# Later sends in the plan, and a third place for activations, in a two-layer attention and mixture-of-experts kernel

## The chip, the cores and the metric

One core of a Trainium2 chip runs the whole program in one launch. The metric is the device time of that core in microseconds (us); lower is better. The engines are TensorE (PE), VectorE (DVE), ScalarE (ACT), GpSimd (POOL) and SyncE (SP), which issues most of the transfers. Each takes its instructions from a queue of its own in a fixed order.

## The reference

The input x has 8 sequences of 512 rows with 128 columns. Two layers follow. In each, attention with 16 heads is added to x and then a mixture of experts. All is float32.

```python
x = x + attn_a(layernorm(x))     # 16 heads, 8 + 32 query and key columns, softmax
x = x + ffn(layernorm(x))
x = x + attn_b(layernorm(x))     # rotary q and k, softmax(q1 k1) - lam * softmax(q2 k2)
x = x + ffn(layernorm(x))

def ffn(x):                      # 8 experts, 512 hidden, the best expert of each row alone
    score = softmax(x @ Wg + bg); e = argmax(score)
    h = silu(x @ W1[e] + b1[e])
    return (h @ W2[e] + b2[e]) * score[e]
```

## The kernel before, in words

**Batches and groups.** A batch b is one sequence in one layer: 16 of them, 0 to 7 for the first attention and 8 to 15 for the second. A batch of the first has 4 groups g and one of the second 8, 96 groups in all. For a group, smax (L1238) computes scores, rowmax on DVE (L1587) their maxima, score (L1259) computes them again transposed, expo on ACT (L1461) exponentiates, pv (L1271) multiplies with the values. The stack stage (SP, L1050) loads a group's q and k from DRAM, the mput stage its maxima. After a batch come normal, join (POOL, L1852), oproj, a second layer norm (ln_stats on DVE, ln_rstd L1810 and ln_apply L1530 mostly on POOL), gating, and scatter (POOL, L1861), which sends rows by indirect transfer to their expert's region in DRAM (`xs`). In the second layer POOL also does the rotary products (turned, L1833 to L1839) and splits into halves (b_lo, L1845).

**Expert blocks.** The 16 batches form four segments (3, 5, 6 and 2 batches). When a segment's batches are scattered, its rows are worked off in blocks m of 128 rows: 19, 27, 31 and 15 blocks, 92 in all (77 before the tail). A block's stages are:

- weights (SP, L1068 and L1063): 576 KB of one expert, into one of seven places WE
- rows (SP, L1105; its waits are at L1104): 128 rows into X, six places. It waits until the send of block m - 6 has landed.
- xturn (PE, L1344), xcopy (ACT, L1491), up (PE, L1352)
- silu_t (ACT, L1500): tanh of up's result into TH; it waits for the down of block m - 2, as Z and TH have two places each
- either on POOL, for the 46 blocks for which `on_pool` holds (segment 1, and segment 2 without its last twelve, the late blocks): silu_z (ACT, L1509) copies up's result into Z, silu_p (POOL, L1868 and L1870) makes two passes over 128x512, down (PE, L1367), weigh (ACT, L1506), plus_p (POOL, L1876)
- or, for the other blocks: silu_b (DVE, L1753), down, combine (DVE, L1760)
- plus_b2 (DVE, L1747), and send (POOL, L1883): an indirect transfer of the 128 finished rows to DRAM (`x2` after layer one, `out` after layer two). It waits for plus_p or combine.

The tail (15 blocks) has six places of Z and TH, in other memory. `mixed` uses the first two places of TH early on, to prepare the experts' weights.

**The order of the work.** It isn't written by hand. `schedule()` is a planner: coroutines (jobs) ask for stages, each with a rank, and the planner places them one at a time. `STAGES` (L193 to L210) holds each stage's engine and planned duration in us, `HOP` what passes until another engine sees the result, `LANDS` how long a transfer takes to land after its issue. For each engine it takes the stage that can start first, with the lower rank on a tie (PE alone weighs rank in, by 0.08 us each), and then the earliest over all engines. Every placement moves the engine's clock, and so what is placed next. Out of it come the orders of the five queues and the PSUM banks, which are then emitted as code; on the chip the engines wait by semaphore and keep these orders, whatever the durations really are. Waits that the plan makes among stages are `after(...)`. In `expert(m)` up is asked for after the down of block m - `back_z`, which is 2 before the tail and 6 in it. Five jobs (lanes) work off the blocks before the tail, block m + 5 after block m's send has been placed. In `step` a stage that follows another of its job on the same engine is ready when that engine is free (`free`), on another engine when the result is seen (`ready`).

Of the kernel before, what the change touches and what calls it, by code (L numbers as in the profile page):

```python
# [7 lines left out]
F32 = mybir.dt.float32  # L8
# [37 lines left out]
M0 = TAIL[0]  # L46
# [101 lines left out]
def weight_slot(m):  # L148

    if m < M0:  # L150
        return m % 7
    return f"t{m - M0}" if m < M0 + 5 else (m - 5) % 7
# [16 lines left out]
def late(m):  # L169

    return M0 - 12 <= m < M0


def on_pool(m):

    return 0 < BLOCKS[m][0] < NS - 1 and not late(m)
# [10 lines left out]
def ends_of_segment(k):  # L187
# [16 lines left out]
    "expo": ("scalar", 0.49), "mcopy": ("scalar", 0.18), "ocopy": ("scalar", 0.49), "hcopy": ("scalar", 0.49), "raw": ("scalar", 0.5), "fhi": ("scalar", 0.585),  # L204
    "vcopy": ("scalar", 0.58), "b_hi": ("scalar", 1.05), "acopy": ("scalar", 0.49), "gcopy": ("scalar", 0.49),
    "gate_exp": ("scalar", 0.25), "silu_z": ("scalar", 0.48), "weigh": ("scalar", 0.265), "plus_p": ("gpsimd", 0.46), "mix": ("vector", 1.4), "wsum": ("tensor", 0.86), "silu_t": ("scalar", 0.49), "lambda_exp": ("scalar", 0.25),
    "index": ("gpsimd", 0.2), "ln_rstd": ("gpsimd", 1.36), "turned": ("gpsimd", 7.4), "silu_p": ("gpsimd", 2.64), "b_lo": ("gpsimd", 2.27), "scatter": ("gpsimd", 4.9), "send": ("gpsimd", 1.0),
    "xload": ("sync", 0.6), "setup": ("sync", 0.6), "put": ("sync", 1.8), "direct": ("sync", 3.6), "stack": ("sync", 1.2), "mput": ("sync", 0.6), "weights": ("sync", 1.1),
    "rows": ("sync", 1.1), "blank": ("sync", 0.6), "fill": ("sync", 9.0), "weights_b": ("sync", 0.6), "weights_p": ("sync", 0.6),
    "wload": ("sync", 1.0), "wstore": ("sync", 0.6),  # L210
# [23 lines left out]
def schedule(ticks=False):  # L234
# [12 lines left out]
    def after(*events):  # L247
        yield ("after", events)

    def do(rank, stage, *index, us=None, engine=None):  # L250
        yield from behind(stage, index)
        yield ("do", rank, stage, index, 0, us, engine)

    def fill_bank(rank, stage, *index, us=None):
        yield from behind(stage, index)
        yield ("do", rank, stage, index, 1, us, None)
# [16 lines left out]
    def find_banks(n, t, stage):  # L273

        kind = stage if stage in MOST else "other"
        held = sum(1 for bank in RB if bank not in idle and (holder[bank][0] if holder[bank][0] in MOST else "other") == kind)
        most = len(RB) if ("scored", (NG - 1,)) in ended else MOST[kind]
        if held >= most:
            return None
        pair, single = free_banks(2) if n == 2 and held + 2 <= most else None, free_banks(1)  # L280
        if single is None:
            return None
        if n == 2 and held > 1 and kind == "smax":
            return pair
        return pair if pair and pair[0] <= max(t, single[0]) else single
# [24 lines left out]
    def give(stage, *index):  # L310
        for bank, _ in ring[stage, index]:
            idle[bank] = ended[LAST[0]]
# [308 lines left out]
    def rank_of(m):  # L621
        k, i = BLOCKS[m]
        return FROM[k][0] + FROM[k][1] * i
# [40 lines left out]
    def lane(ms):  # L664
        for m in ms:
            yield from expert(m)

    def expert(m):
        rank, tail = rank_of(m), BLOCKS[m][0] == NS - 1
        first, back_z = (M0, 6) if tail else (0, 2)  # L670
        if late(m):
            rank = 95.9 + 0.1 * (m - M0 + 12)
            yield from after()
        yield from after(("rows", (m,)), ("weights", (m,)))
        yield from fill_bank(rank, "xturn", m)
        if m >= 4:
            yield from after(("up", (m - 4,)))
        yield from do(rank, "xcopy", m)
        give("xturn", m)
        spawn(plus(m, rank))  # L680
        if m - back_z >= first:
            yield from after(("down", (m - back_z,)))
        yield from fill_bank(rank, "up", m)
        if m == M0:
            yield from after(("pv", (NG - 1, 3)))
        yield from do(rank, "silu_t", m)
        if on_pool(m):
            yield from do(rank, "silu_z", m)
            give("up", m)
            yield from do(rank, "silu_p", m)  # L690
        else:
            yield from do(rank, "silu_b", m)
            give("up", m)
        yield from fill_bank(rank, "down", m)
        yield from after(("plus_b2", (m,)))
        if on_pool(m):
            yield from do(rank, "weigh", m)
            give("down", m)
            yield from do(rank, "plus_p", m)
        else:  # L700
            yield from do(rank, "combine", m)
            give("down", m)
        yield from do(rank, "send", m)

    def plus(m, rank):
        yield from do(rank, "plus_b2", m)
# [6 lines left out]
    def step(job, t):  # L713

        while True:
            ask = next(job, None)
            if ask is None:
                return
            if ask[0] == "do":
                _, rank, stage, index, bank, us, engine = ask  # L720
                engine = engine or STAGES[stage][0]
                before, ready, free = last_of.get(job, (None, 0.0, 0.0))
                t = max(t, free if before == engine else ready)
                asked[engine].append((rank, t, job, stage, index, bank, STAGES[stage][1] if us is None else us))
                return
            events = ask[1] if ask[0] == "after" else (ask[1],)
            missing = [e for e in events if e not in ended]
            if missing:
                blocked.setdefault(missing[0], []).append((job, t, ask))
                return  # L730
            if ask[0] == "after":
                t = max([t] + [ended[e] for e in events])

    def spawn(job):
        step(job, now[0])
# [21 lines left out]
    while any(asked.values()):  # L757
        best = None
        for e in ENGINES:
            mine = None  # L760
            for k, (rank, t, job, stage, index, bank, us) in enumerate(asked[e]):
                if bank:
# [3 lines left out]
                    t = max(t, found[0])  # L766
# [14 lines left out]
        rank, t, job, stage, index, bank, us = asked[e].pop(k)  # L781
        if bank:
            _, first, n = find_banks(bank, max(t, clock[e]), stage)
# [35 lines left out]
def build(nc, a):  # L819
    with ExitStack() as ctx:  # L820
        def sb(name, shape, dt):
            return ctx.enter_context(nc.sbuf_tensor(name, shape, dt))
# [52 lines left out]
        X = sb("X", [128, 6, ROWW], F32)  # L875
        XT = sb("XT", [128, 4, 128], F32)
        WE = sb("WE", [128, 7, WEW], F32)
        Z = sb("Z", [128, 2, 512], F32)
        mean = sb("mean", [128, 128], F32)
        TH = sb("TH", [128, 2, 512], F32)  # L880

        xs = [nc.dram_tensor(f"xs{i}", [NE * REG + 128, ROWW], F32, kind="Internal").ap() for i in range(NS)]
        x2 = nc.dram_tensor("x2", [T, D], F32, kind="Internal").ap()
# [9 lines left out]
        def sem(name):  # L893
            if name not in sems:
                sems[name] = ctx.enter_context(nc.semaphore(name))
            return sems[name]
# [30 lines left out]
        def block_place(m):  # L927

            sk, t, xt_ = STK[:, :].bitcast(F32), m - M0, XT[:, m % 4, :]
            if t < 0:  # L930
                return WE[:, m % 7, :], X[:, m % 6, :], xt_, Z[:, m % 2, :], TH[:, m % 2, :]
            zt = P[:, :, :, :].rearrange("p z j n -> p (z j n)")
            w_ = sk[:, 2412 + WEW * t:2412 + WEW * (t + 1)] if t < 5 else WE[:, weight_slot(m), :]
            return (w_, sk[:, ROWW * (t % NE):ROWW * (t % NE + 1)], xt_, zt[:, 512 * (t % 6):512 * (t % 6) + 512],
                    zt[:, 3072 + 512 * (t % 6):3584 + 512 * (t % 6)])

        def z_before(m):

            return m - 2 if m < M0 else m - 6 if m - 6 >= M0 else None

        def xt_before(m):
            return m - 4
# [33 lines left out]
        def bank_of(stage, *index):  # L976

            return ring[stage, index][0][0], [freed(before[0], *before[1]) for _, before in ring[stage, index] if before]
# [4 lines left out]
        def _(eng):  # L983
# [86 lines left out]
            def wload(e):  # L1070
# [3 lines left out]
                if e >= 7:  # L1074
                    on.wait_ge("wst0", 16)
                eng.dma_start(WE[:, e % 7, :], a["we"][128 * e:128 * e + 128, :]).then_inc(sem(f"wl{e % 2}"), 16)
                eng.dma_start(TH[:, e % 2, :], a["b1"][e].rearrange("(a n) -> a n", a=1).broadcast_to([128, FH])).then_inc(
                    sem(f"wl{e % 2}"), 16)
# [92 lines left out]
        def _(eng):  # L1171
# [169 lines left out]
            def xturn(m):  # L1341
                bank = bank_for("xturn", m)
                on.wait_ge(*x_sem(m))
                eng.transpose(ps[:, bank, 0:128], block_place(m)[1][:, 0:128], idf[:, :]).then_inc(sem("ft"), 1)  # L1344
# [189 lines left out]
        def _(eng):  # L1534
            on = On(eng)

            def mix(e):

                on.wait_ge("ws", e + 1)
                eng.scalar_tensor_tensor(out=TH[:, e % 2, :], in0=TH[:, e % 2, :], scalar=1.0 / 128, in1=ps[:, bank_of("wsum", e)[0], :],  # L1540
                                         op0=ALU.mult, op1=ALU.add).then_inc(sem("mix"), 1)
                on.wait_ge("mix", 2 * e + 1)
                eng.tensor_tensor(WE[:, e % 7, 0:FH], WE[:, e % 7, 0:FH], TH[:, e % 2, :], ALU.add).then_inc(sem("mix"), 1)

# [424 lines left out]
```

## Time and profile before

| | us |
|---|---|
| median of 3 runs | 1557.32 |
| lowest and highest | 1546.62, 1561.79 |
| the profiled execution | 1556.93 |
| its span | 1555.1 |

The span runs from the first to the last instruction of the profiled execution; its mean granted TensorE clock is 0.955 of full speed. Busy time of an engine leaves out what only issues or waits, except that POOL's indirect transfers count. In a row of the timeline the bracket at the end is the idle time of that engine before the instruction, and what ended it.

### The profile page before, as it was taken

The page shows a single profiled execution, that of the slowest core. Times are in us where ns is not written, and L with a number is a line of the kernel's source. Part 1 is how long each engine was busy: PE and PEld are TensorE (multiplying, and loading weights), DVE is VectorE, ACT ScalarE, POOL GpSimd, SP SyncE. Part 2 cuts the span into 40 slices and gives each one's busy share as a digit, 9 for nine tenths or more (in the row PEclk, how much of TensorE's full clock was granted, in tenths as well). Part 3 has the DMA queues.
Part 4 walks back from the last instruction along what each step waited for, and adds up shares of the span by engine and source line. Part 5 has one row for each costly group of instructions (what it writes and reads, how often), then busy time and mean ns, then how long its engine had stood idle before and what let it go on. Part 6 is the DMA issues. An engine that isn't in the chain of part 4 may idle for free.

```text
span 1555.1 us, 26964 instructions
## 1 busy us (share of the span) xinstructions
PE 1404.0 (90%) x9162; PEld 604.7 (39%) x9162; DVE 1186.0 (76%) x2033; ACT 1070.9 (69%) x1960; POOL 677.5 (44%) x744
## 2 busy tenths in 40 slices
PE   7989999999999988889988889889998998889986
PEld 3323334334554322445442323223233323443376
DVE  6757688887778677866669899898988987668563
ACT  3556566676666766778677788787888866767832
POOL 5332344334413861587755543514343123854043
PEclk8999999999999988999899999999999977999998
DMA  2488576865762243545301542211211135533073
GB/s 82 128 263 248 166 226 188 268 189 177 221 189 76 79 145 121 174 143 166 109 28 35 154 140 77 70 34 56 56 42 55 29 100 173 168 120 99 2 252 91
DMA packets 125230, 199.81 MB, mean 128 GB/s; under 512 B 16728, under 2 KB 91186, under 8 KB 125094
## 3 DMA queue, kind: packets, MB, share of 16 engines
q1 hardware_dynamic: 115910, 184.23, 39.8%
q0 software_dynamic: 6016, 12.71, 2.4%
q10 hardware_dynamic: 3168, 1.15, 0.3%
q8 instruction: 74, 1.21, 0.3%
q14 instruction: 62, 0.51, 0.1%
HBM read 123.90 MB, written 72.59 MB: 126 GB/s over the span
## 4 chain that ended last, share of the span: by engine, by line
PE 56%; ACT 11%; POOL 10%; DVE 9%; issue 6%; SPq 3%; DMA 3%; ACTq 1%; another core or an unknown queue 0%; POOLq 0%; DVEq 0%
PE ps L1271 17%; PE ps L1238 10%; PE ps L1259 9%; ACT P L1461 8%; DVE Mb L1587 7%; PE ps L1367 4%; PE ps L1352 3%; PE ps L1204 3%; PE ps L1279 2%; POOL TH L1868 2%; POOL Z L1870 2%; PE ps L1324 1%; POOL x L1883 1%; PE ps L1220 1%; PE ps L1305 1%
## 5 line engine op out<-in xcount | busy, mean ns | idle before, releaser
L1587 DVE TENSOR_REDUCE Mb<-ps 128x2 f32<-128x1024 f32 (+1 forms) x993 | 921.3, 976 | 203.7 <-PE ps L1238 189.7
L1461 ACT ACTIVATE P<-ps 128x512 f32<-128x512 f32 (+1 forms) x1275 | 797.4, 693 | 204.3 <-PE ps L1259 168.0
L1259 PE MATMUL ps<-STK 32*128 32x512 f16 (+1 forms) x1536 | 403.5, 392 | 40.5 <-ACT P L1461 28.0
L1271 PE MATMUL ps<-P,V 128*32 128x512 f32 x3072 | 416.2, 625 | 0.7 <-ACT OR L1468 0.2
L1238 PE MATMUL ps<-STK 32*128 32x512 f16 (+1 forms) x1536 | 371.0, 392 | 35.8 <-ACT P L1461 11.9
L1238 PEld LDWEIGHTS ps<-STK 32*128 32x128 f16 (+1 forms) x1536 | 99.9, 93 | 322.5 <-DVE Mb L1587 104.5
L1259 PEld LDWEIGHTS ps<-STK 32*128 32x128 f16 (+1 forms) x1536 | 108.9, 94 | 225.4 <-ACT P L1461 105.2
L1271 PEld LDWEIGHTS ps<-P,V 128*32 128x32 f32 x3072 | 65.8, 110 | 129.5 <-issue 112.6
L1861 POOL DMA_INDIRECT xs<-ROW,slot x64 | 63.7, 995 | 103.8 <-DVE slot L1678 88.6
L1367 PE MATMUL ps<-WE,Z 128*128 128x128 f32 x616 | 92.5, 297 | 17.7 <-POOL Z L1870 12.8
L1825 POOL CAST HL<-RT 128x512 f16<-128x512 f32 x47 | 28.8, 612 | 171.0 <-ACT RT L1407 150.9
L1367 PEld LDWEIGHTS ps<-WE,Z 128*128 128x128 f32 x616 | 80.7, 204 | 50.2 <-issue 20.9
L1352 PE MATMUL ps<-XT,WE 128*128 128x128 f32 x696 | 97.0, 285 | 3.0 <-ACT XT L1491 1.7
L1352 PEld LDWEIGHTS ps<-XT,WE 128*128 128x128 f32 x696 | 87.5, 197 | 20.6 <-issue 8.2
L1852 POOL TENSOR_TENSOR AT<-AT,OT 128x256 f32<-128x256 f32 x32 | 23.4, 732 | 157.5 <-DVE OT L1610 157.2
L1868 POOL TENSOR_TENSOR TH<-TH,Z 128x512 f32<-128x512 f32 x46 | 58.6, 1274 | 70.9 <-ACT Z L1509 70.1
L1883 POOL DMA_INDIRECT x<-X x46 | 46.3, 1006 | 95.7 <-DVE X L1760 74.3
L1500 ACT ACTIVATE TH<-ps 128x512 f32<-128x512 f32 x77 | 46.2, 601 | 57.1 <-PE ps L1352 50.3
L1204 PE MATMUL ps<-HT,WA 128*128 128x512 f32 x158 | 83.0, 623 | 1.3 <-ACT HT L1390 0.6
L1530 POOL TENSOR_SCALAR ROW<-ROW,mv,rs 128x128 f32<-128x128 f32 x100 | 78.3, 792 | 2.0
L1833 POOL TENSOR_TENSOR RT<-RT,CS 128x512 f32<-128x512 f32 x32 | 40.6, 1276 | 84.2 <-ACT RT L1417 84.0
L1279 PE MATMUL ps<-idf,OR 128*128 128x128 f32 x320 | 53.2, 291 | 9.7 <-ACT P L1461 5.6
(160 smaller groups left out, 1378.8 us busy)
## 6 DMA issues: line engine op xcount, KB each, us to landing
WE<-wx SPq DMA_DIRECT2D x87, 576.0 KB, 4.0
STK<-qka SPq DMA_DIRECT2D x56, 480.0 KB
qka<-HL SPq DMA_DIRECT2D x84, 256.0 KB, 4.8
STK<-qkb SPq DMA_DIRECT2D x64, 256.0 KB
qkb<-HL SPq DMA_DIRECT2D x96, 128.0 KB, 2.7
X<-xs SPq DMA_DIRECT2D x77, 129.5 KB
xs<-pad SPq DMA_DIRECT2D x8, 1036.0 KB
qka<-HL SPq DMA_DIRECT2D x42, 128.0 KB
```

Source lines behind the costliest of these rows:

```text
L1204: eng.matmul(ps[:, bank, :], WA[:, 128 * x:128 * x + 128], HT[:, b % 2, :], start=True, stop=True).then_inc(sem("pr"), 1)
L1238: mm = eng.matmul(ps[:, bank + i, :], l_, r_, start=True, stop=True)
L1259: mm = eng.matmul(ps[:, bank + i, :], l_, r_, start=True, stop=True)
L1271: mm = eng.matmul(ps[32 * j:32 * j + 32, OB, :], V[:, b % 3, kt, at:at + 32], P[:, st % 3, j, :], start=(kt == 0 and (b >= B or hh % 2 == ...
L1279: mm = eng.transpose(ps[:, bank, 128 * i:128 * i + 128], OR[:, 128 * i:128 * i + 128], idf[:, :])
L1352: mm = eng.matmul(ps[:, bank, 128 * c:128 * c + 128], w_[:, 128 * c:128 * c + 128], xt_, start=True, stop=True)
L1367: mm = eng.matmul(ps[:, bank, 0:128], z[:, 128 * c:128 * c + 128], w_[:, FH + D * c:FH + D * c + D], start=(c == 0), stop=(c == 3))
L1461: eng.activation(P[:, st % 3, j:j + n, :], ps[:, bank:bank + n, :], ACT.Exp, scale=SCALE_A if g < 4 * B else SCALE_B).then_inc(sem("exp"), 1)
L1530: eng.tensor_scalar(ROW[:, t0 + i, 0:128], ROW[:, t0 + i, 128:256], mv[:, z, i, 0:1], rs[:, z, i:i + 1], ALU.subtract, ALU.mult).then_inc( ...
L1587: eng.tensor_reduce(Mb[:, g % 2, at:at + 4 * n - 3:4], ps[:, bank:bank + n, :], AX, ALU.max).then_inc(sem("mx"), 1)
L1861: eng.indirect_dma_start(out=xs[k][:, :], out_offset=bass.IndirectOffsetOnAxis(ap=slot[:, t:t + 1], axis=0), in_=ROW[:, t, 0:ROWW], in_off ...
L1868: eng.tensor_tensor(th, th, z, ALU.mult).then_inc(sem("fq"), 1)
```

## The change

Four things change. The planned duration of send goes from 1.0 to 1.2 us. The planner takes a send as ready 0.65 us later than its operand. Z and TH have three places each instead of two for the blocks before the tail (2 KB more for each in every partition). So silu_t waits for the down of block m - 3, and the planner asks for up after that same down. No instruction is added or removed on the chip; the orders of the queues come from a new run of the planner.

```diff
-    ... "send": ("gpsimd", 1.0),
+    ... "send": ("gpsimd", 1.2),
@@ def expert(m)
-        first, back_z = (M0, 6) if tail else (0, 2)
+        first, back_z = (M0, 6) if tail else (0, 3)
@@ def step(job, t)
-                t = max(t, free if before == engine else ready)
+                t = max(t, free if before == engine else ready) + (0.65 if stage == "send" else 0.0)
@@ def build(nc, a)
-        Z = sb("Z", [128, 2, 512], F32)
+        Z = sb("Z", [128, 3, 512], F32)
-        TH = sb("TH", [128, 2, 512], F32)
+        TH = sb("TH", [128, 3, 512], F32)
@@ def block_place(m)
-                return WE[:, m % 7, :], X[:, m % 6, :], xt_, Z[:, m % 2, :], TH[:, m % 2, :]
+                return WE[:, m % 7, :], X[:, m % 6, :], xt_, Z[:, m % 3, :], TH[:, m % 3, :]
@@ def z_before(m)
-            return m - 2 if m < M0 else m - 6 if m - 6 >= M0 else None
+            return m - 3 if m < M0 else m - 6 if m - 6 >= M0 else None
```

## Rows read from the trace of the kernel before

**Rows 1.** The page: busy time of two engines, and POOL's tenths in 40 slices.

```profile
PE 1404.0 (90%) x9162; PEld 604.7 (39%) x9162; DVE 1186.0 (76%) x2033; ACT 1070.9 (69%) x1960; POOL 677.5 (44%) x744
...
POOL 5332344334413861587755543514343123854043
```

**Rows 2.** Busy time by stretch: engines in columns, then PE clock, DMA share, GB/s.

```profile
core 0: us, PE busy (x) PEld busy (x) DVE busy (x) ACT busy (x) POOL busy (x), PEclk, DMA share, GB/s
200.00:350.00 150.00, 147.04 (x845) 57.35 (x847) 125.69 (x239) 102.62 (x165) 55.62 (x66) 1.00 0.72 216
350.00:480.00 130.00, 128.46 (x846) 72.76 (x842) 95.62 (x164) 81.52 (x134) 45.38 (x52) 1.00 0.61 179
636.00:676.00 40.00, 35.35 (x280) 21.03 (x272) 28.38 (x35) 31.85 (x63) 33.12 (x33) 1.00 0.52 159
676.00:706.00 30.00, 25.70 (x178) 13.33 (x178) 19.30 (x26) 21.68 (x40) 25.22 (x25) 0.89 0.43 129
706.00:726.00 20.00, 18.88 (x151) 10.68 (x149) 13.90 (x19) 15.42 (x34) 16.36 (x17) 1.00 0.56 169
...
1302.00:1362.00 60.00, 52.71 (x406) 30.51 (x399) 39.42 (x55) 44.56 (x90) 48.09 (x49) 0.98 0.50 153
```

**Rows 3.** The chain that ended last, by line: 636 to 680, then 1302 to 1362.

```profile
by line: POOL TH L1868 23.2%; POOL Z L1870 23.1%; issue 18.8%; POOL x L1883 16.5%; POOL X L1876 9.1%; PE ps L1352 2.5%; PE ps L1271 2.3%; POOL AT L1852 1.7%; ACT Z L1509 1.3%; ACT TH L1500 1.0%; POOLq L905 0.6%; POOLq L1883 0.6%
...
by line: POOL Z L1870 23.2%; POOL TH L1868 23.1%; issue 17.0%; POOL out L1883 17.0%; POOL X L1876 8.2%; POOL AT L1852 3.7%; PE ps L1271 3.1%; PE ps L1352 2.2%; ACT Z L1509 1.0%; ACT TH L1500 0.7%; PE ps L1344 0.7%; POOLq L905 0.6%; POOLq L1
```

**Rows 4.** Order of time on POOL: start, duration, instruction, idle time before it.

```profile
648.89 1.28 POOL L1868 TENSOR_TENSOR TH<-TH,Z 128x512 f32<-128x512 f32 x1
...
651.48 0.46 POOL L1876 TENSOR_TENSOR X<-X 128x128 f32<-128x128 f32 x1
652.71 1.00 POOL L1883 DMA_INDIRECT x<-X  x1 [0.77 <-POOL X L1876]
653.75 1.28 POOL L1868 TENSOR_TENSOR TH<-TH,Z 128x512 f32<-128x512 f32 x1
```

**Rows 5.** Who waited for whom: us in total, times, longest.

```profile
POOL x L1883 <- POOL X L1876: 18.7, 24, 0.8
...
PE ps L1367 <- POOL Z L1870: 12.8, 16, 2.8
...
POOL out L1883 <- POOL X L1876: 12.8, 16, 0.8
```

**Rows 6.** Order of time on PE, ACT, POOL and SP's queue, 659 to 682.

```profile
659.11 0.27 PE L1344 MATMUL ps<-idf,X 128*128 128x128 f32 x1
...
669.65 0.62 ACT L1509 COPY Z<-ps 128x512 f32<-128x512 f32 x1
...
673.31 1.28 POOL L1868 TENSOR_TENSOR TH<-TH,Z 128x512 f32<-128x512 f32 x1
...
677.12 1.01 POOL L1883 DMA_INDIRECT x<-X  x1 [0.77 <-POOL X L1876]
...
681.51 3.51 SPq L1105 DMA_DIRECT2D X<-xs  x2
```

**Rows 7.** Order of time on POOL: sends that don't follow the stage they wait for.

```profile
407.56 1.11 POOL L1883 DMA_INDIRECT x<-X  x1 [0.18 <-issue]
...
1477.55 0.76 POOL L1852 TENSOR_TENSOR AT<-AT,OT 128x256 f32<-128x256 f32 x1
1478.48 0.99 POOL L1883 DMA_INDIRECT out<-X  x1 [0.17 <-issue]
```

**Rows 8.** What SP's queue waited for at the rows stage.

```profile
SPq L1104 <- DMA x<-X: 47.4, 20, 5.7
SPq L1104 <- DMA out<-X: 31.3, 17, 4.2
```

**Rows 9.** The chain in order of time, late blocks: start, us, what.

```profile
1491.95 3.98 DMA X<-xs
```

**Rows 10.** Groups of instructions by line: xturn on PE.

```profile
L1344 PE MATMUL ps<-idf,X 128*128 128x128 f32 x77 | 21.1, 289 | 1.8 <-DMA X<-xs 1.8
```

More of the change, by code:

```diff
@@ L206 @@
     "gate_exp": ("scalar", 0.25), "silu_z": ("scalar", 0.48), "weigh": ("scalar", 0.265), "plus_p": ("gpsimd", 0.46), "mix": ("vector", 1.4), "wsum": ("tensor", 0.86), "silu_t": ("scalar", 0.49), "lambda_exp": ("scalar", 0.25),
-    "index": ("gpsimd", 0.2), "ln_rstd": ("gpsimd", 1.36), "turned": ("gpsimd", 7.4), "silu_p": ("gpsimd", 2.64), "b_lo": ("gpsimd", 2.27), "scatter": ("gpsimd", 4.9), "send": ("gpsimd", 1.0),
+    "index": ("gpsimd", 0.2), "ln_rstd": ("gpsimd", 1.36), "turned": ("gpsimd", 7.4), "silu_p": ("gpsimd", 2.64), "b_lo": ("gpsimd", 2.27), "scatter": ("gpsimd", 4.9), "send": ("gpsimd", 1.2),
     "xload": ("sync", 0.6), "setup": ("sync", 0.6), "put": ("sync", 1.8), "direct": ("sync", 3.6), "stack": ("sync", 1.2), "mput": ("sync", 0.6), "weights": ("sync", 1.1),
```

## The prediction

> **What bounds the kernel now.** I read the page first. PE is busy for 90% of the span and POOL for 44% [rows 1]. So TensorE looks like the bound and GpSimd like an engine with room. But the digits of the 40 slices show that POOL's share is uneven: it is 8, 7, 7 tenths in the slices from about 660 to 780 us and 8 again around 1320 to 1360, which are the stages in which the expert blocks of segments 1 and 2 run beside attention. Those are the blocks that the change touches, so the second view is busy time by stretch [rows 2]. In the two stretches before the third stage, 200 to 350 us and 350 to 480 us (there segment 0 runs its blocks on VectorE), PE is busy for 98.0% and 98.8%: nothing is to be had. In 636 to 676 us PE falls to 35.35 of 40 us (88%), in 676 to 706 to 25.70 of 30 (86%), in 706 to 726 to 18.88 of 20 (94.4%), in 1302 to 1362 to 52.71 of 60 (88%). POOL is busy for 33.12 of 40 and 48.09 of 60 there.
>
> The third view is the chain that ended last, cut to these stretches [rows 3]: from 636 to 680 us POOL's own lines and "issue" make up over 90% of it, and the same from 1302 to 1362. The fourth is POOL's order of time [rows 4]. One turn is silu_p (L1868, L1870), plus_p (L1876), send (L1883), from the silu_p at 648.89 to the next at 653.75: 4.86 us. In it POOL stands still for 0.77 us between plus_p, which writes the rows, and the send that waits for them. The whole list of waits has 24 + 16 = 40 such gaps, 18.7 + 12.8 = 31.5 us, and PE waits at down (L1367) for POOL's Z 16 times, 12.8 us [rows 5]. So in these stretches the bound is a saturated POOL, in front of a PE with some 12% to spare.
>
> **The change, part by part.** Two edits are to the planner. A send is planned at 1.2 us instead of 1.0, and as ready 0.65 us after its operand. The old plan has a send begin at once behind its plus_p, at 2.64 + 0.46 + 1.0 = 4.10 us for a block; the chip takes 4.86. The new plan sees, at the end of plus_p, a send that is ready only 0.65 us later; any other POOL stage that is ready before that is placed first. What is that? In the trace the next block's silu_p: its Z was copied at 669.65 to about 670.27, two turns ahead of need by the order, and POOL comes to it at 673.31, behind a send (1.00 us and its gap of 0.77) [rows 6]. Without that send POOL would come at 671.5, so Z is ready in time with two places already, by about 1 us, and with three places easily, as its up no longer waits for the down just made. I expect the order silu_p, send of the block before, plus_p.
>
> What is the gap then? The trace has sends whose operand was long there and that follow some other instruction; two of them show 0.18 and 0.17 us idle [rows 7]. The two ends for the gap in the new place are thus 0.17 (a saving of 0.60) and 0.77 (no saving, if the lead belongs to the send itself); I take 0.20, by these rows, the nearest in kind: a saving of 0.57 us for each.
>
> A rule speaks against this. The Trainium skill, "Perfetto Trace Analysis", section "DMA Instruction — SWDGE (GPSIMD)", says that such an instruction has no start marker, only an end, when the last DSP has made its descriptors. By that the 0.77 us could be part of the send's own work and would move with it: no saving, 1557. What the trace shows goes against it: from the end of plus_p at about 651.94 to the next silu_p at 653.75 are 1.81 us, while the send at 1478.48 ends 1.16 us after the join before it ended [rows 4, 7].
>
> How many gaps count? In 636 to 676 there are 7, in 676 to 706 4, in 706 to 726 4, in 1302 to 1362 11: 26 of the 40. The other 14 lie where POOL waits for ACT or stands beside a PE that is already full, and I cost them at nothing; PE's work hides them. For the 26, POOL gives 4.0, 2.3, 2.3 and 6.3 us. What is late next is PE: at the 98% of [rows 2] its 35.35 us need 36.1, so at most 3.9 us go; in 706 to 726 at most 0.7; in 1302 to 1362 52.71 need 53.8, at most 6.2. In 676 to 706 the long rotary stages stand on POOL's chain and half of 2.3, 1.1, is what I count. Sum 11.9 us. If PE gets only to the 94.4% that it had in 706 to 726, the terms are 2.6, 1.1, 0 and 4.2: 7.9 us. I take the middle, 9.9.
>
> The third place of Z and TH. On the blocks on POOL it is what lets up and tanh run a block ahead; priced above. On the 19 blocks of segment 0 it is worth nothing, since PE is full there (98.8%). On the twelve late blocks the chain shows a row load of 3.98 us at 1491.95 [rows 9], which a place of Z doesn't shorten: between 0 and 4 us (if an earlier up hid it all), taken as 0, since the row names the load. The tail already has six places.
>
> The later send. It frees X's slot (six of them) for the rows of six blocks on, and SP stands for it in its one queue: 20 + 17 waits, 47.4 + 31.3 us [rows 8]. One block followed through: xturn at 659.11, its send at 677.12, and the rows that take its slot are issued from 681.51, 4.4 us after the send; add 4 us to land [rows 9]: 685.5, a life of 26.4 us [rows 6]. Six turns of 4.86 are 29.2. The new order adds a silu_p, 2.6 us, and the six turns shrink by 6 x 0.57 = 3.4; that asks for 6.0 where 2.8 is free behind the rows. The rest has to come out of the waits inside the life (Z stands 3.0 us before silu_p takes it, 670.27 to 673.31, and part of the time between xturn and up is a wait too). They hold about the 3.2 us that are missing, hence a cost of 0; the other end is the whole gain lost.
>
> All other order is planned anew too, as each placement moves those behind it. No row prices that; the three times of before span 1546.6 to 1561.8, so a plan that is a little better or worse somewhere is hard to tell from a run. I leave it at 0 with 8 us to either side.
>
> **Sum.** The profiled execution took 1556.93 us (span 1555.1), the median of the runs shown is 1557.32, so both stand for the same. 1556.9 - 9.9 = 1547.0 us.
>
> **The rivals.**
> (a) No gain, by X's ring or PE. If the waits inside a block's life don't shrink, the turn is (26.4 + 2.6) / 6 = 4.83 us, what it is now. The same comes out if the send stays behind its plus_p, or if the lead is the send's own and moves with it (the Trainium skill's missing start marker, above); that alone I hold for 0.05 of the 0.22. For it: SP's 37 waits for a send. Against it: PE waited at xturn (L1344) for X's rows for 1.8 us in the whole trace [rows 10]. Time 1556.
> (b) The plan fits, and all 40 gaps count: 40 x 0.57 = 22.8 us, with PE's 16 waits for Z inside that. For it: the old plan was 0.76 us a block too fast, so everything that it put behind was late too. Against it: the PE limit above. Time 1534.
> (c) Slower: SP's queue. Each rows stage waits until its send has landed, some 2 us later than now, and behind it on SP stand the stack (the q and k of a later group, L1050) and the weights (L1068). It decides when the stack's slack is used up: in the two stages, 320 us together, some 23 groups start (the second layer's 64 take about 870 us, 13.6 each); if for each smax is 2 us late and none of POOL's gain is left, that is 46 us, if for half, 23. Against it: the planner places the stack 3.4 groups ahead of its use, some 40 us at the pace of the second layer, and 2 us of that matter little. Time 1556.9 + 23 = 1580.
>
> **How the numbers follow.** Forecast 0.53, (a) 0.22, (b) 0.13, (c) 0.12. The forecast's own range is 1539 to 1555 with the replanning. Leaving out the outer half of (c) and a little of (b), the range is 1532 to 1566. One per cent, 15.6 us, is about what a measurement of this kernel tells from no change, given its spread: faster means under 1541.7. To that go (b) and about two fifths of the forecast, 0.34. Slower, over 1572.9, is most of (c): 0.10. The rest is 0.56.
>
> **What would show it.** Right: POOL's order of time around 640 to 680 us has send behind silu_p with 0.2 us idle before it; the waits of L1883 for POOL's X fall from 40 to a few; a turn takes 4.3 to 4.5 us; PE is busy for 94 to 98% from 636 to 676 and from 1302 to 1362; the last send to x2 comes earlier. Wrong: a gap of 0.7 us before a send that follows silu_p (the lead is the send's own); turns of 4.8 us with xturn waiting for rows (a); SP's waits at L1104 well over 80 us and DVE or PE waiting for a stack (c); or turns as forecast and the time unchanged, with PE's idle time moved to 750 to 850 or to the end.

## The result, and the profile after

The changed kernel takes 1515.31 us in the median of 4 runs (1514.28 to 1524.05). The kernel before, run beside it, has a median of 1553.37 (4 runs). The ratio is 0.9759, 95% interval 0.9719 to 0.9800: faster by 2.4%. The forecast was 1547.0 us (0.994), with a range from 1532 to 1566, so the time lies outside the range, on the faster side. The profiled execution took 1515.25 us; its span is 1513.4, 41.7 us less than that of before.

The page of the changed kernel, busy time by engine and POOL's tenths in 40 slices:

```profile
PE 1382.8 (91%) x9162; PEld 594.7 (39%) x9162; DVE 1188.0 (78%) x2046; ACT 1070.1 (71%) x1958; POOL 678.6 (45%) x744
...
POOL 5332334424422764387865643414433133964143
```

Beside [rows 1], POOL's, DVE's and ACT's busy times are the same to within 2 us. PE's is 21.2 us shorter with the same 9162 matmuls. PE's idle time went from 1555.1 - 1404.0 = 151.1 to 1513.4 - 1382.8 = 130.6 us, 20.5 us less. So the gain has two halves, and my working has terms only for the second. Part of the first half belongs to the two executions and not to the kernels: the profiled one of before had a mean granted clock of 0.955, that of the changed kernel 0.970, and the last section shows what such a difference goes with in one kernel.

The step of the forecast that was about POOL came out as written. Order of time on POOL, changed kernel (start, duration, instruction, idle time before it), which answers to [rows 4]:

```profile
637.99 1.27 POOL L1868 TENSOR_TENSOR TH<-TH,Z 128x512 f32<-128x512 f32 x1
639.34 1.27 POOL L1870 TENSOR_TENSOR Z<-Z,TH 128x512 f32<-128x512 f32 x1
640.76 1.01 POOL L1883 DMA_INDIRECT x<-X  x1
641.79 0.47 POOL L1876 TENSOR_TENSOR X<-X 128x128 f32<-128x128 f32 x1
642.20 1.28 POOL L1868 TENSOR_TENSOR TH<-TH,Z 128x512 f32<-128x512 f32 x1
```

The send stands behind the next block's silu_p, 0.15 us after it, and a turn takes 4.21 us where it took 4.86. The waits of the changed kernel (us, times, longest), which answer to [rows 5] and [rows 8], and the group of xturn, to [rows 10]:

```profile
POOL x L1883 <- POOL X L1876: 3.9, 5, 0.8
...
POOL out L1883 <- POOL X L1876: 0.8, 1, 0.8
```

```profile
SPq L1104 <- DMA x<-X: 46.0, 17, 8.2
SPq L1104 <- DMA out<-X: 37.1, 15, 4.8
```

```profile
L1344 PE MATMUL ps<-idf,X 128*128 128x128 f32 x77 | 21.8, 293 | 0.6 <-DMA X<-xs 0.3 <-ACT Z L1509 0.2
```

Six gaps are left of 40. The wait of down for POOL's Z, 12.8 us before, is not in the list any more. SP stands 83.1 us for sends instead of 78.7, and PE waits for X's rows for 0.3 us: X's ring held.

The chain that ended last, changed kernel, from 628 to 672 us, then from 1274 to 1340 ([rows 3] before), and busy time in two stretches at the head of the two stages ([rows 2]):

```profile
by line: PE ps L1352 20.8%; PE ps L1367 17.1%; PE ps L1271 14.5%; DVE Mb L1587 13.5%; PE ps L1238 7.0%; DVE X L1747 6.4%; issue 5.8%; PE ps L1259 5.6%; PE ps L1344 2.1%; PE ps L1279 2.0%; PE ps L1204 2.0%; ACT P L1461 1.4%; PE ps L1244 1.1%
...
by line: PE ps L1367 23.3%; PE ps L1352 20.2%; PE ps L1271 19.4%; PE ps L1238 11.0%; PE ps L1259 7.4%; ACT P L1461 4.8%; DVE Mb L1587 2.9%; ACT TH L1500 2.2%; PE ps L1344 2.2%; PE ps L1279 2.2%; ACT Z L1509 1.6%; issue 1.2%; PE ps L1244 0.9
```

```profile
628.00:668.00 40.00, 38.41 (x299) 21.31 (x295) 32.23 (x45) 34.07 (x69) 37.05 (x36) 1.00 0.50 151
1284.00:1344.00 60.00, 57.44 (x453) 31.28 (x451) 46.03 (x64) 49.26 (x100) 50.90 (x54) 1.00 0.57 171
```

POOL is gone from the chain and PE has taken its place, busy for 96.0% and 95.7% where it was at 88%; I had written 94 to 98%.

**Where the other half lies.** To compare the same work in two traces I cut them at the ACT copies L1468, which end the groups. There is one for every group of the second layer and one for every two of the first, so number 15 (of 80, counted from 0) is the last of layer one. The copies with the numbers 15, 31, 63, 71 and 79 bound four stretches. Three of them in the kernel before (segment 1's stage, the middle, the first part of segment 2's stage), then in the changed kernel:

```profile
core 0: us, PE busy (x) PEld busy (x) DVE busy (x) ACT busy (x) POOL busy (x), PEclk, DMA share, GB/s
568.77:847.69 278.92, 245.19 (x1700) 113.74 (x1696) 202.03 (x327) 200.10 (x387) 166.75 (x174) 0.90 0.38 120
847.69:1227.91 380.22, 342.86 (x2466) 112.68 (x2465) 341.65 (x543) 312.16 (x583) 146.98 (x151) 1.00 0.25 72
1227.91:1373.66 145.75, 128.24 (x850) 57.52 (x847) 105.47 (x176) 99.53 (x196) 68.98 (x71) 0.87 0.42 130
```

```profile
565.35:820.40 255.05, 230.37 (x1683) 107.85 (x1679) 201.35 (x340) 197.24 (x387) 162.13 (x168) 0.95 0.43 131
820.40:1204.28 383.88, 350.35 (x2485) 113.04 (x2483) 345.35 (x551) 315.73 (x596) 151.71 (x157) 0.99 0.25 71
1204.28:1329.84 125.56, 116.12 (x828) 53.07 (x825) 101.95 (x166) 95.91 (x196) 67.34 (x68) 0.93 0.47 144
```

Segment 1's stage is 23.9 us shorter: PE idles 9.1 us less and is busy 14.8 us less. Segment 2's is 20.2 us shorter: 8.1 us of idle time and 12.1 of busy time. The middle gives 3.7 us back: PE is busy there for 7.5 us more, with 19 more matmuls, so a part of the shorter busy time is work that has moved to another stretch. In both stages the granted clock is higher, 0.90 to 0.95 and 0.87 to 0.93. The clock doesn't sag evenly: it drops to half speed (1.2 GHz) for some microseconds. One such drop in the kernel before, 4 us a line:

```profile
752.00:756.00 4.00, 2.81 (x18) 0.64 (x18) 2.44 (x4) 3.26 (x7) 4.00 (x5) 0.89 0.18 45
756.00:760.00 4.00, 3.90 (x20) 1.25 (x19) 2.28 (x3) 1.69 (x5) 3.92 (x6) 0.50 0.55 156
760.00:764.00 4.00, 4.00 (x21) 3.16 (x21) 2.25 (x7) 2.46 (x5) 2.06 (x2) 0.50 0.01 1
764.00:768.00 4.00, 4.00 (x28) 1.21 (x27) 1.72 (x5) 2.86 (x5) 1.56 (x2) 0.50 0.35 94
768.00:772.00 4.00, 4.00 (x37) 3.47 (x38) 1.23 (x9) 1.98 (x5) 1.27 (x2) 0.90 0.56 172
```

Before it PE was busy for only 2.81 of 4 us, while POOL was busy for 4.00 of 4; afterwards PE is full and slow for some 12 us. What PE waited for just before the drop, and what ACT had waited for:

```profile
752.35 0.38 PE L1259 MATMUL ps<-STK 32*128 32x512 f16 x1 [0.92 <-ACT Z L1509]
753.72 0.39 PE L1238 MATMUL ps<-STK 32*128 32x512 f16 x1 [0.84 <-ACT P L1461]
...
750.18 1.14 ACT L1424 CAST HL<-RT 128x512 f16<-128x512 f32 x2 [1.06 <-POOL RT L1839]
```

So PE waited for ACT here, and ACT a little earlier for POOL's rotary products, not for a block's silu_p or send. The changed kernel has two such drops after 620 us in segment 1's stage where the kernel before has four. Before all four PE waited for ACT, and in two of them (688 and 752 us) ACT had waited for POOL's rotary products.

### The profile page after: what moved, and what is told of

Its sections match the earlier page's. It is cut to its first block, busy times and chain, and to the rows that moved or that the text cites. A ratio compares the mean times of both kernels' runs of the same rounds, so it can differ in the third digit from the quotient of the medians.

```text
span 1513.4 us, 26975 instructions
## 1 busy us (share of the span) xinstructions
PE 1382.8 (91%) x9162; PEld 594.7 (39%) x9162; DVE 1188.0 (78%) x2046; ACT 1070.1 (71%) x1958; POOL 678.6 (45%) x744
## 4 chain that ended last, share of the span: by engine, by line
PE 66%; DVE 11%; ACT 11%; issue 5%; SPq 2%; POOL 2%; DMA 2%; ACTq 1%; another core or an unknown queue 0%; POOLq 0%; DVEq 0%
PE ps L1271 19%; PE ps L1259 11%; PE ps L1238 11%; DVE Mb L1587 9%; ACT P L1461 7%; PE ps L1367 6%; PE ps L1352 6%; PE ps L1204 3%; PE ps L1279 2%; PE ps L1220 1%; PE ps L1324 1%; PE ps L1305 1%; ACT OR L1468 1%; PE ps L1244 1%; PE ps L1344 1%
## 5 line engine op out<-in xcount | busy, mean ns | idle before, releaser
L1587 DVE TENSOR_REDUCE Mb<-ps 128x1 f32<-128x512 f32 (+1 forms) x1006 | 922.9, 966 | 167.4 <-PE ps L1238 159.6
L1259 PE MATMUL ps<-STK 32*128 32x512 f16 (+1 forms) x1536 | 395.3, 388 | 34.6 <-ACT P L1461 20.2
L1271 PE MATMUL ps<-P,V 128*32 128x512 f32 x3072 | 409.4, 615 | 1.0 <-ACT OR L1468 0.2
L1367 PE MATMUL ps<-WE,Z 128*128 128x128 f32 x616 | 89.4, 290 | 6.9 <-issue 3.0
L1367 PEld LDWEIGHTS ps<-WE,Z 128*128 128x128 f32 x616 | 77.4, 197 | 36.2 <-issue 15.9
```

Source lines behind the costliest of these rows:

```text
L1259: mm = eng.matmul(ps[:, bank + i, :], l_, r_, start=True, stop=True)
L1271: mm = eng.matmul(ps[32 * j:32 * j + 32, OB, :], V[:, b % 3, kt, at:at + 32], P[:, st % 3, j, :], start=(kt == 0 and (b >= B or hh % 2 == ...
L1367: mm = eng.matmul(ps[:, bank, 0:128], z[:, 128 * c:128 * c + 128], w_[:, FH + D * c:FH + D * c + D], start=(c == 0), stop=(c == 3))
L1587: eng.tensor_reduce(Mb[:, g % 2, at:at + 4 * n - 3:4], ps[:, bank:bank + n, :], AX, ALU.max).then_inc(sem("mx"), 1)
```

## The experiments

Each ran in 4 to 10 executions beside the kernel before on the same chip; the ratios are to that. Their intervals reach 0.003 to 0.008 to either side. Theory A is that POOL's gap was on the path and its going is the gain, B that the new plan of all queues gains, C that the third place does.

**The sends alone, in both directions.** `swap` keeps all orders of the kernel before and, after planning, moves on POOL each send that stands right behind its plus_p one stage back:

```diff
         order, ring = schedule()
+        late_sends, i = order["gpsimd"], 1
+        while i < len(late_sends) - 1:
+            (s0, x0), (s1, x1), (s2, x2_) = late_sends[i - 1:i + 2]
+            if s0 == "plus_p" and s1 == "send" and x0 == x1 and s2 in ("silu_p", "join", "turned"):
+                late_sends[i], late_sends[i + 1] = late_sends[i + 1], late_sends[i]
+                i += 1
+            i += 1
```

> The kernel before with all its orders kept, except that on POOL each send that stood right behind its own plus_p changes places with the stage behind it (silu_p, join or turned). Theory A (the idle 0.77 us between plus_p and send lay on the path): turns of about 4.2 us instead of 4.86 and most of the gain, a ratio of 0.976 to 0.985. Theory B (the new plan of all five queues is what gains, by its order on PE): at most a third of the gain, 0.992 to 1.000. Theory C (the third place gains): 0.997 to 1.003.

`unswap` is the inverse, on the changed kernel:

```diff
         order, ring = schedule()
+        sends = [x for x in order["gpsimd"] if x[0] == "send" and on_pool(x[1][0])]
+        rest = [x for x in order["gpsimd"] if x not in sends]
+        order["gpsimd"] = [y for x in rest for y in ([x, ("send", x[1])] if x[0] == "plus_p" else [x])]
```

> The changed kernel with all its orders and three places kept, except that on POOL each send of a block on POOL is put back right behind its plus_p. Theory A: the gap of 0.77 us and turns of 4.86 us are back and most of the gain is gone, a ratio of 0.990 to 1.000 to the kernel before. Theory B: 0.976 to 0.983, as the changed kernel. Theory C: the same, 0.976 to 0.983.

Measured: swap 0.9880 (0.9799 to 0.9960), 1534.46 us. unswap 0.9919 (0.9880 to 0.9959), 1538.87 us. For unswap theory A's range held and those of B and C didn't; swap fell between the ranges of A and B. Neither theory had it whole. POOL's order in swap, then in unswap (the lines of the file are a few higher):

```profile
642.72 1.27 POOL L1877 TENSOR_TENSOR Z<-Z,TH 128x512 f32<-128x512 f32 x1
644.14 1.01 POOL L1890 DMA_INDIRECT x<-X  x1 [0.15 <-issue]
645.18 0.47 POOL L1883 TENSOR_TENSOR X<-X 128x128 f32<-128x128 f32 x1
645.60 1.27 POOL L1875 TENSOR_TENSOR TH<-TH,Z 128x512 f32<-128x512 f32 x1
```

```profile
655.38 1.27 POOL L1873 TENSOR_TENSOR Z<-Z,TH 128x512 f32<-128x512 f32 x1
656.62 0.45 POOL L1879 TENSOR_TENSOR X<-X 128x128 f32<-128x128 f32 x1
657.85 1.01 POOL L1886 DMA_INDIRECT x<-X  x1 [0.77 <-POOL X L1879]
658.89 1.29 POOL L1871 TENSOR_TENSOR TH<-TH,Z 128x512 f32<-128x512 f32 x1
```

The gap of 0.77 us is tied to the place behind plus_p, under either plan. What down on PE waited for POOL's Z (us, times, longest), swap, then unswap, 12.8 us before:

```profile
PE ps L1374 <- POOL Z L1877: 1.3, 2, 1.1
...
PE ps L1370 <- POOL Z L1873: 12.2, 13, 3.3
```

So with two places too Z comes in time once the sends are moved. And the same stretch between copies 15 and 31, swap, then unswap:

```profile
567.84:827.17 259.33, 232.02 (x1700) 109.56 (x1696) 206.30 (x327) 198.78 (x387) 166.64 (x174) 0.96 0.42 129
```

```profile
569.34:845.74 276.40, 243.06 (x1683) 110.94 (x1679) 203.72 (x340) 197.90 (x387) 162.35 (x168) 0.90 0.40 121
```

Moving the sends alone takes 19.6 us out of this stage under the old plan; putting them back adds 21.4 us under the new. In both PE's busy time goes with them (245.2 to 232.0, and 230.4 to 243.1), and so does the clock, 0.90 without the move and 0.95 or 0.96 with it. These are the two pairs in which the stage moves most; the seven pairs below, and this line of the same stage in replan_b3, a new plan of the kernel before with 38 of the 40 gaps still in it, show that the clock isn't tied to the gaps alone:

```profile
568.02:820.14 252.12, 223.38 (x1678) 105.65 (x1674) 203.52 (x340) 194.95 (x381) 164.90 (x169) 0.99 0.43 132
```

Over the whole kernel the move is worth 0.012 in one plan and 0.016 in the other. The rest of the change, at either place of the sends, is worth 0.008 to 0.012.

**The edits apart.** `plan` has the two planner edits and two places; `places` the three places with the old planner (its weights stage also waits for plus_b2 of the block that held the place of WE).

```diff
 plan:    the 1.2 and the + (0.65 if stage == "send" else 0.0) of the change, nothing else
 places:  back_z, Z, TH, block_place and z_before of the change, and in weights(m)
+                    on.wait_ge("fbp" if on_pool(weight_before(m)) else "fb", nth(weight_before(m)))
```

> The two edits of the planner alone (send ready 0.65 us later and planned at 1.2 us), Z and TH with two places. Theory A: Z was ready about 1 us ahead of POOL with two places, so the new order holds and nearly all of the gain comes, 0.976 to 0.985. Theory C (the third place is needed to let up run ahead): less than half of it, 0.988 to 1.000. Theory B doesn't say: another plan, another time.

> The third place of Z and TH alone (with it the weights stage also waits for plus_b2 of the block that held its place, which this order needs), the planner's send as before. Theory A: POOL's turn stays 4.86 us with its gap of 0.77 us, so 0.995 to 1.003. Theory C: most of the gain, 0.976 to 0.985.

Measured: plan 0.9875 (0.9811 to 0.9940), between the ranges of A and C, and places 1.0073 (1.0034 to 1.0113). With two places the planner's edits leave 13 of the 40 gaps. The third place alone makes the kernel slower, a result outside both expectations; beside plan it seems worth 0.012. It wasn't quite alone: at helper line L905 SP stands in places for plus_b2, 27.4 us in three waits, 26.5 of them between 1400 and 1460 us, a wait that the kernel before doesn't have. What that costs isn't separated. A part worth +0.007 alone and -0.012 in company raised the question what any new plan does to the time.

**New plans that cheapen nothing.** Each is one small number in the table of planned durations; on the chip no instruction is added, removed or changed.

```diff
 replan_b1 (before), replan_a1 (change):  "index": ("gpsimd", 0.2)  -> 0.25
 replan_b2 (before), replan_a2 (change):  "join": ("gpsimd", 0.73)  -> 0.70
```

> The kernel before, planned anew with another duration for one small stage of POOL (index at 0.25 us instead of 0.2), which makes nothing on the chip cheaper. It measures what a new plan alone is worth. Theory A (the gap on POOL and what follows from it) expects 0.995 to 1.005. Theory B (a new plan of all queues can gain a per cent by luck) expects replanned kernels to scatter by 0.01 or more to either side.

> The kernel before, planned anew with join at 0.70 us instead of 0.73. Theory A: 0.995 to 1.005. Theory B: another draw of the same scatter, 0.01 or more from 1 in one of the two.

> The changed kernel, planned anew with index at 0.25 us instead of 0.2. Theory A: the gain stays, 0.972 to 0.980 to the kernel before. Theory B: part of the gain was the luck of one plan, and it falls to 0.983 to 0.990 here or in the other one.

> The changed kernel, planned anew with join at 0.70 us instead of 0.73. Theory A: 0.972 to 0.980. Theory B: 0.983 to 0.990 here or in the other one.

| | ratio | interval |
|---|---|---|
| replan_b1 | 0.9953 | 0.9918 to 0.9987 |
| replan_b2 | 1.0046 | 1.0000 to 1.0092 |
| replan_a1 | 0.9969 | 0.9931 to 1.0008 |
| replan_a2 | 1.0076 | 1.0040 to 1.0111 |

The two replans of before stay inside theory A's range (0.995 to 1.005). The two of the change lie outside both theories' ranges (0.972 to 0.980, and 0.983 to 0.990), on the slow side. The change, planned anew with 0.05 us more for a stage that runs 16 times, loses nearly all of its gain; with join at 0.70 it ends slower than the kernel before. In both, POOL's sends are still moved (9 and 12 of 40 gaps are left). Where does replan_a2 lose it? Its segment 1 stage is nearly as short as the change's (the first line), but the stretch between copies 71 and 79, at the end of segment 2's blocks, takes 119.79 us (the second):

```profile
570.05:829.95 259.90, 234.58 (x1698) 109.67 (x1694) 205.39 (x346) 197.65 (x383) 166.01 (x172) 0.96 0.43 129
1349.46:1469.25 119.79, 105.86 (x732) 46.06 (x729) 75.78 (x124) 84.28 (x165) 41.87 (x46) 0.90 0.25 74
```

The changed kernel needs 101.01 us for it:

```profile
1329.84:1430.85 101.01, 93.04 (x686) 38.24 (x686) 73.00 (x115) 81.16 (x153) 38.28 (x43) 0.97 0.29 87
```

There PE idles 13.9 us instead of 8.0, and runs at 0.90 of its clock instead of 0.97. A further 12.1 us go in the stretch before it, copies 63 to 71: 137.68 us, where the changed kernel takes 125.56. In the places kernel the stretch between copies 71 and 79 is as long, 118.15 us. From copy 79 to the end all kernels take 81 to 86 us, whatever went before.

**The same move under four more plans.** swap_b1 and swap_b2 are replan_b1 and replan_b2 with the edit of swap; unswap_a1 and unswap_a2 are replan_a1 and replan_a2 with the edit of unswap; unswap_plan is plan with it.

> replan_b1 with only POOL's sends moved behind the stage after their plus_p, as in swap. Theory A' (moving the sends gains the same under any plan, about 0.012 to 0.016 of the time, and the rest of the change's gain is the draw of the plan): 0.9953 - 0.014, so 0.978 to 0.985. Theory B (everything is the draw; the move and its gain in swap were an accident of that plan): 0.992 to 1.000.

> replan_b2 with only POOL's sends moved in the same way. Theory A': 1.0046 - 0.014, so 0.987 to 0.994. Theory B: 1.000 to 1.010.

> replan_a1 with only POOL's sends put back right behind their plus_p. Theory A': 0.9969 + 0.014, so 1.007 to 1.014. Theory B: 0.992 to 1.002.

> replan_a2 with only POOL's sends put back right behind their plus_p. Theory A': 1.0076 + 0.014, so 1.018 to 1.025. Theory B: 1.003 to 1.012.

> plan (the planner's edits, two places) with only POOL's sends put back right behind their plus_p. Theory A' (the move gains in any plan where POOL is on the path; mean of the five pairs so far 0.009): 0.9875 + 0.005 to 0.016, so 0.992 to 1.004. Theory B (only the draw): 0.984 to 0.991.

The last two columns are from the profiled execution of each: how much less PE idles, and how much less it is busy, with the sends moved, in the stretches between copies 15 and 31 and between copies 63 and 71 together.

| plan | sends behind plus_p | sends moved | the move gains | PE idle less, us | PE busy less, us |
|---|---|---|---|---|---|
| before / swap | 1.0000 | 0.9880 | 0.0120 | 13.9 | 14.8 |
| replan_b1 / swap_b1 | 0.9953 | 0.9865 | 0.0088 | 2.3 | -1.5 |
| replan_b2 / swap_b2 | 1.0046 | 0.9992 | 0.0054 | 4.4 | 3.5 |
| unswap / the change | 0.9919 | 0.9759 | 0.0160 | 12.8 | 11.8 |
| unswap_a1 / replan_a1 | 1.0074 | 0.9969 | 0.0105 | 10.0 | -7.4 |
| unswap_a2 / replan_a2 | 1.0080 | 1.0076 | 0.0004 | 13.8 | 8.0 |
| unswap_plan / plan | 0.9940 | 0.9875 | 0.0065 | 9.2 | 6.2 |

No pair goes the other way. The mean is 0.0085, and the seven scatter by 0.005 around it, so 0.004 to 0.013 with 95%: 13 us. Theory A' was right in sign and too high in size: its range held for unswap_a1 and unswap_plan and was missed on the low side by the other three, of which unswap_a2 lies in theory B's range. Theory B doesn't hold for the mean of the seven, but in one plan of seven the move is worth nothing that can be seen.

PE's idle time in the two stages falls in all seven, by 9.5 us in the mean (5.2 to 13.7 with 95%). Its busy time falls by 5.1 us in the mean, with an interval from -2.0 to 12.2: over plans, no busy time is shown to go with the sends.

**More draws.** plan_b1 and plan_b2 are plan with index at 0.25 and join at 0.70; replan_a3 and replan_a4 are the change with index at 0.15 and join at 0.76; replan_b3 is the kernel before with index at 0.15.

> The planner's edits with two places, planned anew with index at 0.25 us. Theory P (the third place is worth nothing; plans with two and three places are draws of the same spread): the mean of plan, plan_b1 and plan_b2 lies within 0.007 of 0.9935, the mean of the change and its two replans. Theory C (the third place gains): their mean lies above 1.000.

> The planner's edits with two places, planned anew with join at 0.70 us. Theories P and C as for plan_b1; by P a single value may lie anywhere from 0.976 to 1.008.

> The change, planned anew with index at 0.15 us. Theory L (the change's own plan is a lucky draw, by about 0.015): 0.985 to 1.008. Theory S (the edits themselves gain 0.02 or more, and replan_a1 and replan_a2 were the unlucky ones): 0.972 to 0.982.

> The change, planned anew with join at 0.76 us. Theory L (lucky draw): 0.985 to 1.008. Theory S (the edits themselves gain 0.02 or more): 0.972 to 0.982.

> The kernel before, planned anew with index at 0.15 us. Theory L: a draw around 1.000, 0.990 to 1.010. If it lies at 0.985 or below, draws as good as the change's are had without its edits, and nothing of the gain beyond the moved sends can be given to them.

| planner's send, places | ratios | mean |
|---|---|---|
| as before, two | 1.0000, 0.9953, 1.0046, 0.9882 | 0.9970 |
| as changed, two | 0.9875, 0.9849, 0.9854 | 0.9859 |
| as changed, three | 0.9759, 0.9969, 1.0076, 0.9843, 0.9850 | 0.9899 |

replan_a3 and replan_a4 fall on the edge of theory L's range (0.9843 and 0.9850, where it begins at 0.985) and outside theory S's. replan_b3, 0.9882 (0.9812 to 0.9951), is a better draw than the range expected of it (0.990 to 1.010). The mean of plan, plan_b1 and plan_b2 is 0.9859, just under theory P's range (0.9865 to 1.0005) and far from theory C's (above 1.000). The five plans of the change have a standard deviation of 0.012; its own is the best of them, 0.014 below their mean. All eight plans with the changed send average 0.9884, 0.0086 below the four without. With this scatter that difference alone has an interval from -0.003 to 0.020; it agrees with the pairs, which show it far better. The third place doesn't show: with it 0.9899, without it 0.9859, and that difference is within the scatter. By ratio no other kernel of the study beat the change.

## Why the prediction was wrong

**Right.** POOL's gap and its price: 0.77 us behind plus_p, 0.15 behind silu_p (I took 0.20), 40 gaps reduced to 6. Z ready in time with two places: swap shows it, where PE's wait for POOL's Z falls to 1.3 us. PE as what is late next, at 96%, and a turn a little shorter than I wrote (4.21 us; I had 4.3 to 4.5). X's ring and SP's queue as covers that hold, so rivals (a) and (c) fell. The rule of the Trainium skill that I weighed against the change ("Perfetto Trace Analysis", section "DMA Instruction — SWDGE (GPSIMD)", no start marker) decided nothing: the trace and the pairs show that the idle time depends on what stands ahead of the send. The size too, taken over plans: 9.9 us forecast, 13 us measured for the move (0.0085, 0.004 to 0.013), and 9.5 us for the idle time of PE in the two stages, the only part that the sum counts.

**The step that failed** is "All other order is planned anew too ... I leave it at 0 with 8 us to either side". That term was mis-sized. Replans that change nothing else run from 0.984 to 1.008, and the plans scatter with a standard deviation of 0.007 for the kernel before and 0.012 for the change, 11 and 19 us, where I had 8 at most. In the change's own plan it came out as 0.008 (1 - 0.9919, by unswap; the interval is 0.004 to 0.012), 13 us, and in the same plan the move was worth 0.016, 25 us where the sum has 9.9, at the top of its seven. The two make the 37 us. Either one alone would have left the time inside the range or at its edge (1556.9 - 9.9 - 13 = 1534, or 1556.9 - 25 = 1532); that both came out on the fast side is the luck of this plan, the best of five. I called this unmeasurable because the runs of before spread by 15 us; but a spread of runs averages out in a median, and one plan's luck doesn't.

**The second step**, shown only in part, is "What is late next is PE: at the 98% of [rows 2] its 35.35 us need 36.1". I took PE's busy time as fixed work and allowed only its idle time to go. The idle time fell by 9.1 and 8.1 us in the two stages, 17 us against the 11.9 at the upper end of my sum, and the busy time by 14.8 and 12.1 us more. That busy time isn't fixed is shown: down's matmuls in the kernel before, from 757 to 767 us at a granted clock of mostly 0.50, and from 640 to 648 at 1.00 (us in total, mean ns of one):

```profile
L1367 PE MATMUL ps<-WE,Z 128*128 128x128 f32 x8 | 2.1, 438 | 0.0
...
L1367 PE MATMUL ps<-WE,Z 128*128 128x128 f32 x24 | 3.4, 283 | 0.0
```

My own rows had the sign of it, a PEclk of 0.89 at 676 to 706 in [rows 2], and I read only the busy columns. What is not shown is that the moved sends bring the clock back. In segment 1's stage swap has 13.2 us less busy time than the kernel before, and the change 12.7 us less than unswap, but swap_b1 has 3.9 us more than replan_b1, and the mean of the seven pairs isn't clear of zero. Right before the drops PE waited for ACT and not for a block's Z. So this half of the gain in the two profiles stays partly open: the clock of the two executions, the plan and the move all enter.

Rival (b), 1534 us, was nearest, but its reason isn't shown: nearly half of the gain is the rest of the plan or its scatter, and whether the gaps outside the four stretches paid wasn't tried apart. There are more of them than the 14 that I named: all 46 sends of the blocks on POOL stood behind their plus_p with at least 0.77 us of idle time, the list of waits puts 40 of these down to POOL's X, and my 26 were counted out of the 46. Of the list's 40, 21 lie in the four stretches and 12 in segment 1's stage after 726 us.

**Open.** Why the move gains 0.016 in one plan and nothing in another isn't settled. Nor is what makes the stretch before copy 79 long in replan_a2 and places; that both have two more blocks in it than the change (11 instead of 9, counted by XT copies on ACT that start in it, and 80 and 88 of up's matmuls instead of 49) fits, but it wasn't tried alone.

## What to carry to other kernels

A kernel whose queues come from a planner has a draw in every edit to the planner: before giving an edit its gain, run two or three plans that differ by a number that means nothing, and test the mechanism by moving it alone in a finished order. An indirect send behind its own producer on the same engine cost 0.6 us more idle time here than one with a stage of other work between them. And a matmul's time isn't fixed: beside every sum of busy time, look at the granted clock of the same rows, and compare several pairs before giving a difference of the clock to one edit.

## What the runs showed of the hardware

An indirect transfer on POOL that waits for the instruction right ahead of it starts 0.77 to 0.81 us after that one ends (45 of 46 in the kernel before; the other, 3.0 us). Right behind another compute stage it starts after 0.14 to 0.20 us when its operand is there, and right behind another indirect transfer after 0.30. The stage between can be as short as join, in the changed kernel:

```profile
671.24 0.46 POOL L1876 TENSOR_TENSOR X<-X 128x128 f32<-128x128 f32 x1
671.65 0.72 POOL L1852 TENSOR_TENSOR AT<-AT,OT 128x256 f32<-128x256 f32 x1
672.53 1.01 POOL L1883 DMA_INDIRECT x<-X  x1 [0.15 <-issue]
```

This send starts 0.83 us after its plus_p has ended, hardly later than without join, so POOL's own work can take nearly the whole lead.

The spread of one kernel's runs goes with the clock. Over 91 executions of the kernel before, span and mean granted clock have a correlation of -0.94: the median span is 1555.1 us where the clock was 0.953 to 0.955, and 1537.8 us where it was 0.970 to 0.972; a line through all has 11 us for 0.01. The profiled execution that the forecast was made from had 0.955, at the slow end; the four of the change had 0.966 to 0.974. Put at one clock by that slope, 0.965, the spans are some 1543 us for the kernel before and some 1522 us for the change, an estimate from its four executions. That is 1.4%: by this about two fifths of the measured gain come with the clock.
